# Loads and stores of a streaming kernel in one DMA queue instead of two

## The chip, the cores and the metric

The kernel runs on one core of one Trainium2 chip. The metric is device time in microseconds (us), the median of several runs. Before the change it is 168.21 us (three runs, 167.97 to 169.08). The change is judged by the same metric.

## The reference

A tensor `x` of 128 samples by 128 steps by 512 features (f32, 33.6 MB) is multiplied by a factor per sample and feature. The factor comes from a small network over the sample's condition vector (512 features):

```python
h = jax.nn.silu(cond @ W1.T + b1)
gate = jax.nn.sigmoid(h @ W2.T + b2)[:, None, :]
# a Haar transform of x over the steps, every coefficient times gate, the inverse transform: x * gate
x = x + (x + x * gate)          # = x * (2 + gate)
```

The transform is orthonormal and the gate does not depend on the step, so transform and inverse cancel, and what is left is `out = x * (2 + gate)`. `x` is read once and `out` written once.

## The kernel before, in words

`x` is cut into 16 chunks: two groups (`GROUPS`, 64 samples each) by eight (`SLOTS`) of 8 steps (`CHUNK_STEPS`). A sample's 128 steps are split over two partitions, so a chunk is 128 partitions by 8 steps by 512 features, 2,048 KB, with 16 KB in a row in each partition and in HBM. The tile `ring` has eight slots, one for each chunk of a group. A chunk is loaded into its slot, multiplied there in place, and stored from there. The second group uses the same eight slots again.

- SyncE (SP) issues the loads. First the weights and the condition rows (lines 100 to 102), then all eight loads of group 0 with no wait (line 104), then the eight loads of group 1 (line 109), the load of slot s after a wait for the store of slot s in group 0 (`chunk_stored[s]`).
- ScalarE (ACT) issues the two bias loads (lines 165 and 166), runs the sigmoids (lines 171 and 176), and then issues all sixteen stores (line 182), each after a wait for VectorE's count `chunk_scaled`. At its end it waits for the last stores (line 185).
- TensorE (PE) transposes the condition and the weights and makes the two matrix products (lines 126 to 160), and VectorE (DVE) copies between them and makes `factor` (line 211).
- VectorE then multiplies the sixteen chunks in order (line 218), each after its load has landed (`chunk_loaded[s]`), and counts up `chunk_scaled`.

Loads and stores so go into two DMA queues, one that SP fills (q1 in the profile) and one that ACT fills (q10). Within a queue the transfers are taken in the order of issue. Between the two nothing in the program orders them but the semaphores.

Of the kernel before, what the change touches and what calls it, by code (L numbers as in the profile page):

```python
# [1 line left out]

# [8 lines left out]
CHUNK_STEPS = 8  # L31
GROUPS = 2
SLOTS = 8
DMA_DONE = 16


def gated_residual_program(nc, x, cond, w1, b1, w2, b2, out):
    B, N, D = x.shape
    BLOCKS = D // P
    SAMPLES = B // GROUPS  # L40
    assert B == P and D == BLOCKS * P and N == GROUPS * SLOTS * CHUNK_STEPS and GROUPS >= 2

    x_parts = x.rearrange("(g q) (h n) d -> g (q h) n d", g=GROUPS, h=GROUPS)
    out_parts = out.rearrange("(g q) (h n) d -> g (q h) n d", g=GROUPS, h=GROUPS)

    with ExitStack() as ctx:
        def sbuf(name, shape):
            return ctx.enter_context(nc.sbuf_tensor(name, shape, F32))
# [4 lines left out]
        def sem(name):  # L53
            return ctx.enter_context(nc.semaphore(name))


        ring = sbuf("ring", [P, SLOTS, CHUNK_STEPS, D])

# [27 lines left out]
        gate_summed, gate_set, factor_set = sem("gate_summed"), sem("gate_set"), sem("factor_set")  # L86
        chunk_loaded = [sem(f"chunk_loaded{s}") for s in range(SLOTS)]
        chunk_scaled = sem("chunk_scaled")
        chunk_stored = [sem(f"chunk_stored{s}") for s in range(SLOTS)]

        block = ctx.enter_context(nc.Block())

        def chunk(parts, g, s):

            return parts[bass.ds(g, 1), :, s * CHUNK_STEPS:(s + 1) * CHUNK_STEPS, :].rearrange("g p n d -> (g p) n d")

        @block.sync
        def _(sp):

            sp.dma_start(w1_rows[:, :, :], w1.rearrange("(p t) k -> p t k", t=BLOCKS)).then_inc(w1_loaded, DMA_DONE)  # L100
            sp.dma_start(cond_rows[:, :], cond).then_inc(cond_loaded, DMA_DONE)
            sp.dma_start(w2_rows[:, :, :], w2.rearrange("(t p) k -> p t k", p=P)).then_inc(w2_loaded, DMA_DONE)
            for s in range(SLOTS):
                sp.dma_start(ring[:, s, :, :], chunk(x_parts, 0, s)).then_inc(chunk_loaded[s], DMA_DONE)
            with sp.Fori(1, GROUPS) as g:
                for s in range(SLOTS):

                    sp.wait_ge(chunk_stored[s], g * DMA_DONE)
                    sp.dma_start(ring[:, s, :, :], chunk(x_parts, g, s)).then_inc(chunk_loaded[s], DMA_DONE)

        @block.gpsimd
        def _(pool):
# [50 lines left out]
        @block.scalar  # L163
        def _(act):
            act.dma_start(b1_cols[:, :], b1.rearrange("(p t) -> p t", t=BLOCKS)).then_inc(b1_loaded, DMA_DONE)
            act.dma_start(b2_row[:, :], b2.rearrange("(a j) -> a j", a=1)).then_inc(b2_loaded, DMA_DONE)

            act.wait_ge(b1_loaded, DMA_DONE)
            act.wait_ge(hidden_summed, 1)
            for t in range(BLOCKS):  # L170
                act.activation(hidden_sigmoid[:, t, :], hidden_sum[:, t, :], ACT.Sigmoid,  # L171
                               bias=b1_cols[:, t:t + 1]).then_inc(sigmoid_set, 1)

            for g in range(GROUPS):
                act.wait_ge(gate_summed, g + 1)
                act.activation(gate[:, g, :], gate_sum[g][:, :], ACT.Sigmoid).then_inc(gate_set, 1)  # L176

            with act.Fori(0, GROUPS) as g:
                for s in range(SLOTS):

                    act.wait_ge(chunk_scaled, g * SLOTS + (s + 1))
                    act.dma_start(chunk(out_parts, g, s), ring[:, s, :, :]).then_inc(chunk_stored[s], DMA_DONE)

            for s in range(SLOTS):
                act.wait_ge(chunk_stored[s], GROUPS * DMA_DONE)

        @block.vector
        def _(dve):

# [51 lines left out]
```

## Time and profile before

| | us |
|---|---|
| median of the runs | 168.21 |
| runs, lowest to highest | 167.97 to 169.08 |
| span of the profiled execution | 166.7 |
| VectorE busy in it | 78.3 |
| TensorE busy in it | 23.7 |
| ScalarE busy in it | 3.6 |
| bytes moved by DMA | 69.47 MB, mean 417 GB/s |

The profiled execution is one run of the program, and its span goes from the first to the last instruction. The median of the runs is 1.5 us above it. Busy time of an engine is the time in which it executes, without waits and without the issuing of DMAs. The page divides the span into 40 slices, 4.17 us each, and gives for each slice the busy share of the 16 DMA engines and the GB/s that they moved. A chain of waits follows the work that ended last back from its end.

### The profile page before, as it was taken

What the parts mean: (1) busy time and instruction counts of PE and PEld (TensorE: products, weight loads), DVE (VectorE), ACT (ScalarE), POOL (GpSimd) and SP (SyncE); (2) the same over time, 40 slices, a digit from 0 to 9 for tenths busy, and PEclk for the clock granted to TensorE, in tenths of its full rate; (3) what the DMA queues carried; (4) which work ended last, traced back from release to release, by engine and by line L of the source; (5) the groups of instructions that cost most, each with busy time, mean ns of one, the idle gap of its engine ahead of it and who ended that gap; (6) DMA issues with size and microseconds to landing.
All of it is one profiled execution on the core that took longest, in us unless ns stands there. A gap on an engine that the chain in (4) does not pass through costs nothing.

```text
span 166.7 us, 361 instructions
## 1 busy us (share of the span) xinstructions
PE 23.7 (14%) x88; PEld 15.6 (9%) x88; DVE 78.3 (47%) x30; ACT 3.6 (2%) x7; POOL 0.8 (1%) x7
## 2 busy tenths in 40 slices
PE   0479619960000000000000000000000000000000
PEld 0479613320000000000000000000000000000000
DVE  0160180019999999997809154280915428000000
ACT  0000500110000000000000000000000000000000
POOL 2000000000000000000000000000000000000000
PEclk9999965997555555555555555555555555555555
DMA  5999999999999999999999999999999999999995
GB/s 167 313 457 440 421 421 429 433 437 433 413 437 429 429 437 440 425 425 429 437 429 437 433 425 433 429 433 433 437 433 425 433 429 429 437 433 433 429 429 236
DMA packets 5570, 69.47 MB, mean 417 GB/s; under 512 B 705, under 2 KB 705, under 8 KB 1346
## 3 DMA queue, kind: packets, MB, share of 16 engines
q1 hardware_dynamic: 3120, 35.91, 51.3%
q10 hardware_dynamic: 2450, 33.56, 47.1%
HBM read 35.92 MB, written 33.55 MB: 417 GB/s over the span
## 4 chain that ended last, share of the span: by engine, by line
DMA 41%; DVE 26%; PE 13%; ACT 2%; issue 2%; SPq 0%; DVEq 0%; ACTq 0%
DMA out<-ring 27%; DVE ring L218 22%; DMA ring<-in_x 11%; PE gate_sum L160 5%; PE hidden_sum L140 3%; DMA cond_rows<-in_cond 3%; PE turned L132 2%; PE gate_sum L157 2%; DVE w_t L208 1%; DVE hidden L201 1%; ACT L171 1%; ACT hidden_sigmoid L171 1%; PE turned_cond L126 1%; DVE factor L211 0%; DVE w_t L194 0%
## 5 line engine op out<-in xcount | busy, mean ns | idle before, releaser
L218 DVE TENSOR_TENSOR ring<-ring,factor 128x4096 f32<-128x4096 f32 x16 | 70.1, 4421 | 33.3 <-DMA ring<-in_x 33.0
L160 PE MATMUL gate_sum<-w_t,hidden 128*128 128x512 f32 x16 | 8.8, 702 | 0.0
L211 DVE TENSOR_SCALAR factor<-gate 128x1024 f32<-128x1024 f32 x1 | 0.7, 694 | 12.6 <-ACT gate L176 12.6
L140 PE MATMUL hidden_sum<-cond_t,w_t 128*128 128x128 f32 x32 | 5.5, 351 | 0.9 <-DVE w_t L194 0.9
L201 DVE SCALAR_TENSOR_TENSOR hidden<-hidden_sum,b_cols,hidden_sigmoid 128x256 f32<-128x256 f32 x4 | 1.7, 478 | 8.3 <-ACT hidden_sigmoid L171 8.3
L140 PEld LDWEIGHTS hidden_sum<-cond_t,w_t 128*128 128x128 f32 x32 | 5.3, 264 | 1.2 <-issue 1.2
L191 DVE COPY cond_t<-turned_cond 128x512 f32<-128x512 f32 x1 | 0.7, 692 | 7.8 <-PE turned_cond L126 7.8
L160 PEld LDWEIGHTS gate_sum<-w_t,hidden 128*128 128x128 f32 x16 | 3.5, 229 | 6.0 <-issue 6.0
L157 PE MATMUL gate_sum<-b_row,ones_row 1*128 1x512 f32 x4 | 3.2, 881 | 4.9 <-DVE w_t L208 4.9
L132 PE MATMUL turned<-identity,w_rows 128*128 128x128 f32 x16 | 3.6, 421 | 0.0
L132 PEld LDWEIGHTS turned<-identity,w_rows 128*128 128x128 f32 x16 | 3.4, 230 | 0.0
L194 DVE COPY w_t<-turned 128x512 f32<-128x512 f32 x4 | 2.8, 692 | 0.6 <-PE turned L132 0.6
L208 DVE COPY w_t<-turned 128x512 f32<-128x512 f32 x4 | 2.5, 681 | 0.0
L149 PE MATMUL turned<-identity,w_rows 128*128 128x128 f32 x16 | 2.1, 283 | 0.0
L126 PE MATMUL turned_cond<-identity,cond_rows 128*128 128x128 f32 x4 | 1.1, 428 | 6.6 <-DMA cond_rows<-in_cond 6.6
L149 PEld LDWEIGHTS turned<-identity,w_rows 128*128 128x128 f32 x16 | 2.0, 208 | 0.0
L171 ACT ACT_TABLE_LOAD x1 | 1.3, 1283 | 17.6 <-PE hidden_sum L140 17.6
L176 ACT ACTIVATE gate<-gate_sum 128x512 f32<-128x512 f32 x2 | 1.2, 597 | 15.5 <-PE gate_sum L160 15.5
L157 PEld LDWEIGHTS gate_sum<-b_row,ones_row 1*128 1x128 f32 x4 | 0.8, 244 | 5.8 <-issue 5.8
L126 PEld LDWEIGHTS turned_cond<-identity,cond_rows 128*128 128x128 f32 x4 | 0.7, 216 | 6.6 <-issue 6.6
L171 ACT ACTIVATE hidden_sigmoid<-hidden_sum,b_cols 128x128 f32<-128x128 f32 x4 | 1.1, 368 | 0.0
L117 POOL TENSOR_SCALAR_AFFINE_SELECT identity<-identity 128x128 f32<-128x128 f32 x1 | 0.3, 294 | 0.1
(6 smaller groups left out, 0.8 us busy)
## 6 DMA issues: line engine op xcount, KB each, us to landing
ring<-in_x SPq DMA_DIRECT2D x16, 2048.0 KB, 18.2
out<-ring ACTq DMA_DIRECT2D x16, 2048.0 KB, 34.8
w_rows<-in_L_cond_W SPq DMA_DIRECT2D x2, 1024.0 KB, 6.8
cond_rows<-in_cond SPq DMA_DIRECT2D x1, 256.0 KB, 5.3
b_cols<-in_L_cond_b ACTq DMA_DIRECT2D x1, 2.0 KB, 5.2
b_row<-in_L_cond_b ACTq DMA_DIRECT2D x1, 2.0 KB
```

Of the source, the lines that this page charges most:

```text
L126: last = pe.transpose(turned_cond[:, c * B:(c + 1) * B], cond_rows[:, c * P:(c + 1) * P], identity[:, :])
L132: last = pe.transpose(turned[c][:, t * P:(t + 1) * P], w1_rows[:, t, c * P:(c + 1) * P], identity[:, :])
L140: last = pe.matmul(hidden_sum[:, t, :], w1_t[:, c, t, :], cond_t[:, c, :], start=(c == 0), stop=(c == BLOCKS - 1))
L149: last = pe.transpose(turned[t][:, m * P:(m + 1) * P], w2_strided[:, m, t, :], identity[:, :])
L157: pe.matmul(gate_sum[g][:, :], ones_row[:, :], b2_row[:, :], start=True, stop=False)
L160: last = pe.matmul(gate_sum[g][:, :], samples, w2_t[:, t, :], start=False, stop=(t == BLOCKS - 1))
L171: act.activation(hidden_sigmoid[:, t, :], hidden_sum[:, t, :], ACT.Sigmoid, bias=b1_cols[:, t:t + 1]).then_inc(sigmoid_set, 1)
L176: act.activation(gate[:, g, :], gate_sum[g][:, :], ACT.Sigmoid).then_inc(gate_set, 1)
L194: dve.tensor_copy(w1_t[:, c, :, :].rearrange("k t p -> k (t p)"), turned[c][:, :]).then_inc(w1_t_set, 1)
L201: dve.scalar_tensor_tensor(out=hidden[:, t, :, :], in0=hidden_sum[:, t, :].unsqueeze(2).to_broadcast([P, B, GROUPS]), scalar=b1_cols[:, t: ...
L208: dve.tensor_copy(w2_t[:, t, :], turned[t][:, :]).then_inc(w2_t_set, 1)
L218: dve.tensor_tensor(ring[:, s, :, :], ring[:, s, :, :], factor_steps, ALU.mult).then_inc(chunk_scaled, 1)
```

## The change

All sixteen stores move from ACT's queue to SP's. SP issues them in a list written out in Python instead of a loop on the engine. For each chunk i it waits until chunk i is multiplied and issues its store. From the third store on, until all eight loads of group 1 are out, it then waits until store i - 2 has landed and issues the load that goes into that slot. The wait for the last stores moves from ACT to SP. ACT keeps the two bias loads and its activations. VectorE, TensorE and GpSimd are unchanged, and so are the sizes and number of the transfers.

```diff
+BEHIND = 2
@@ sync
             for s in range(SLOTS):
                 sp.dma_start(ring[:, s, :, :], chunk(x_parts, 0, s)).then_inc(chunk_loaded[s], DMA_DONE)
-            with sp.Fori(1, GROUPS) as g:
-                for s in range(SLOTS):
-
-                    sp.wait_ge(chunk_stored[s], g * DMA_DONE)
-                    sp.dma_start(ring[:, s, :, :], chunk(x_parts, g, s)).then_inc(chunk_loaded[s], DMA_DONE)
+            chunks = GROUPS * SLOTS
+            for i in range(chunks):
+                sp.wait_ge(chunk_scaled, i + 1)
+                sp.dma_start(chunk(out_parts, i // SLOTS, i % SLOTS),
+                             ring[:, i % SLOTS, :, :]).then_inc(chunk_stored[i % SLOTS], DMA_DONE)
+
+                j = i - BEHIND
+                if j >= 0 and j + SLOTS < chunks:
+                    sp.wait_ge(chunk_stored[j], DMA_DONE)
+                    sp.dma_start(ring[:, j, :, :],
+                                 chunk(x_parts, 1 + j // SLOTS, j % SLOTS)).then_inc(chunk_loaded[j], DMA_DONE)
+
+            for s in range(SLOTS):
+                sp.wait_ge(chunk_stored[s], GROUPS * DMA_DONE)
@@ scalar
-            with act.Fori(0, GROUPS) as g:
-                for s in range(SLOTS):
-
-                    act.wait_ge(chunk_scaled, g * SLOTS + (s + 1))
-                    act.dma_start(chunk(out_parts, g, s), ring[:, s, :, :]).then_inc(chunk_stored[s], DMA_DONE)
-
-            for s in range(SLOTS):
-                act.wait_ge(chunk_stored[s], GROUPS * DMA_DONE)
```

## Rows read from the trace of the kernel before

**Rows 1.** The page: span, busy time of the engines, DMA share and rate by slice.
```profile
span 166.7 us, 361 instructions
PE 23.7 (14%) x88; PEld 15.6 (9%) x88; DVE 78.3 (47%) x30; ACT 3.6 (2%) x7; POOL 0.8 (1%) x7
...
DMA  5999999999999999999999999999999999999995
GB/s 167 313 457 440 421 421 429 433 437 433 413 437 429 429 437 440 425 425 429 437 429 437 433 425 433 429 433 433 437 433 425 433 429 429 437 433 433 429 429 236
```

**Rows 2.** The page: DMA queues with packets, MB, share of the 16 engines.
```profile
q1 hardware_dynamic: 3120, 35.91, 51.3%
q10 hardware_dynamic: 2450, 33.56, 47.1%
```

**Rows 3.** The chain of waits, its last pieces: start us, length us, what.
```profile
72.72 45.41 DMA out<-ring
118.13 0.02 issue
118.15 18.24 DMA ring<-in_x
136.39 0.02 issue
136.41 4.42 DVE ring L218
```

**Rows 4.** Who waited for whom, VectorE and SP's queue: us in total, times, longest.
```profile
DVE ring L218 <- DMA ring<-in_x: 33.0, 7, 5.3
...
SPq L109 <- DMA out<-ring: 108.8, 8, 47.4
```

**Rows 5.** Three stretches: busy us by engine, TensorE clock, DMA share, GB/s.
```profile
16.00:42.00 26.00, 15.19 (x50) 7.47 (x48) 8.95 (x10) 3.62 (x7) 0.00 (x0) 0.82 1.00 427
62.00:134.00 72.00, 0.00 (x0) 0.00 (x0) 41.45 (x10) 0.00 (x0) 0.00 (x0) 0.50 1.01 431
144.00:162.00 18.00, 0.00 (x0) 0.00 (x0) 0.00 (x0) 0.00 (x0) 0.00 (x0) 0.50 1.01 432
```

**Rows 6.** The issues of line 104, and how long they took to land.
```profile
L104 SPq DMA_DIRECT2D ring<-in_x x8: 434/482/877, 2.1 to 6.3; - x8
...
DMA to landing us min/median/max: 13.1/28.1/46.9
```

**Rows 7.** The issues of line 109 and of line 182: duration ns, first and last start.
```profile
L109 SPq DMA_DIRECT2D ring<-in_x x8: 327/328/328, 54.3 to 118.2; - x8
...
L182 ACTq DMA_DIRECT2D out<-ring x16: 337/338/389, 42.4 to 141.0; - x16
```

**Rows 8.** VectorE in order of time, multiplies of line 218: start us, busy us.
```profile
37.79 39.11 DVE L218 TENSOR_TENSOR ring<-ring,factor 128x4096 f32<-128x4096 f32 x9 [0.33 <-DVE factor L211]
...
87.81 4.42 DVE L218 TENSOR_TENSOR ring<-ring,factor 128x4096 f32<-128x4096 f32 x1 [5.30 <-DMA ring<-in_x]
...
136.41 4.42 DVE L218 TENSOR_TENSOR ring<-ring,factor 128x4096 f32<-128x4096 f32 x1 [5.28 <-DMA ring<-in_x]
```

**Rows 9.** DMA in the last 3 us, in 40 slices of 0.075 us from 164.
```profile
GB/s 218 437 437 437 218 874 437 437 218 0 219 0 0 0 0 0 219 0 0 0 0 0 0 0 0 0 0 0 0 0 0 0 0 0 0 0 0 0 0 0
DMA packets 35, 0.31 MB, mean 104 GB/s; under 512 B 16, under 2 KB 16, under 8 KB 16
```

**Rows 10.** ACT's waits for the last stores, line 185: duration ns, first and last start.
```profile
L185 ACTq EVENT_SEMAPHORE  x4: 17/38/38, 151.6 to 166.2; - x4
```

## Prediction, made before the changed kernel was run

> **What bounds the kernel now.** I read the page first. VectorE is busy for 78.3 of 166.7 us and TensorE for 23.7, but the DMA share stands at 9 in every slice between the first and the last [rows 1]. So no compute engine sets the time. The 16 DMA engines do. Next come the queues: 35.91 MB in q1 and 33.56 MB in q10, together 98.4% of all the time that the 16 engines have in the span [rows 2]. The third view is the table of three stretches, chosen so that each shows one regime: loads alone in one queue (16 to 42 us), loads and stores side by side in two queues (62 to 134), stores alone in one queue (144 to 162). They moved 427, 431 and 432 GB/s at a DMA share of 1.00 to 1.01 [rows 5]. The reader should see that rate depends hardly at all on direction, or on whether one queue or two are served.
>
> The chain of waits confirms this in its own way. Its last long pieces are a store of 45.41 us, a load of 18.24 us and one multiply [rows 3]. A transfer of 2.097 MB takes 2.097 / 431 = 4.87 us when it has the engines to itself, so those pieces are mostly time spent standing in a queue. The waits say the same: VectorE waits 33.0 us for loads and SP waits 108.8 us for stores [rows 4], and neither wait leaves the DMA engines idle. They are consequences of the full DMA.
>
> **The fixed part.** The first slice moved at 167 GB/s, the second at 313, and the last at 236 [rows 1]. This start and end hold what the kernel loses against a steady rate. At the start stand the same loads of weights, biases and conditions in the same queues, and the change touches none of them. The last slice ends with the last store and its landing, which the change keeps too.
>
> **The change part by part.**
>
> *Who issues.* Sixteen issues of 0.34 us leave ACT and go to SP, where the same kind takes 0.33 us [rows 7]. SP then has 24 issues after the first eight loads, 24 x 0.33 = 8 us over more than 110 us. SP now waits 108.8 us [rows 4], and this is the cover. If it were gone the 8 us would still lie beside transfers of 4.87 us each. ACT has nothing left behind its gates, so no engine waits for it. I cost this at 0. The closing wait of line 185 moves from ACT to SP, with the same 0.04 us [rows 10]: 0.
>
> *The order of the transfers.* Call the group 0 loads L0 to L7, the stores S0 to S15, and the loads of group 1 N0 to N7. SP's queue becomes L0 to L7, S0, S1, S2, N0, S3, N1, S4, and so on to S9, N7, S10, then S11 to S15. I walk through it to find a place where the DMA engines could run dry. The first load lands at 2.1 + 13.1 = 15.2 us [rows 6], and the others follow at 2.097 / 427 = 4.91 us each, so L7 ends at 15.2 + 7 x 4.91 = 49.6. The first store is issued at 42.4 [rows 7], and VectorE delivers another every 39.11 / 9 = 4.35 us [rows 8], so S1 is issued at 46.7 and S2 at 51.1. S0 is in the queue 7 us before its turn. It runs from 49.6 to 54.4, S1 to 59.3, S2 to 64.1.
>
> *The new waits.* SP waits for S0 from about 51.4 to 54.4, and behind that wait stand N0 and S3. At that moment S1 and S2 are still in the queue, 9.7 us of work. SP issues N0 at 54.4 and S3 at 55.4, when chunk 3 is multiplied. In the same way N1 goes out at 59.3 with S2, N0 and S3 (14.6 us) before it, and from S2's landing at 64.1 on there are always four transfers, about 19.4 us, between the transfer that SP waits for and the load that it then issues. One wait only would have to be late by over 9.7 us, and the later ones by 14 to 19 us, before the engines had nothing. Loads of the second group: N0 ends at 64.1 + 4.9 = 69.0 and the next ones every 9.77 us, so N7 ends at 69.0 + 7 x 9.77 = 137.4. Now its multiply starts at 136.41 [rows 8]. Its product is ready at about 137.4 + 4.4 = 141.8 us, and S15's turn comes only after S10 to S14, at 137.4 + 5 x 4.86 = 161.7, so 20 us of cover remain. S10 itself needs chunk 10, which is multiplied before 95 us. No stall arises, and none disappears: the DMA engines were full before and are full after.
>
> *The rate.* What remains is whether the same bytes pass at the same rate. Now a pair of a load and a store takes (136.41 - 87.81) / 5 = 9.72 us [rows 8]. In the new order the two run one after the other, each at the rate of its own regime: 2.097 / 427 + 2.097 / 432 = 4.91 + 4.85 = 9.76 us [rows 5], 0.04 us more. Over the eight pairs that is 0.3 us. If the group 1 loads run at the mixed rate instead, it is 0.
>
> *The turns.* The trace of before shows no change from stores to loads inside one queue, and the new order has 17: one at L7 to S0, and two for each of N0 to N7. The nearest row below is the mixed stretch, in which load and store packets of two queues share each DMA engine at a DMA share of 1.01 and 431 GB/s [rows 5], so those turns cost nothing there. It could not be much less than nothing, since a share of 1.01 leaves no gap that could be closed, and the best regime is 432. The far end is an engine that lets the writes of one kind be confirmed before it goes on with the other: the last packet starts in the slice at 164 + 16 x 0.075 = 165.2 us [rows 9], though packets of the bulk stop near 164.7, and the wait for the last store starts at 166.2 [rows 10], which leaves at most 1.0 us for the rest of a packet and the confirmation. Of that 1.0 us about 0.6 is the packet (16 KB on one engine, 16,384 B / (431 / 16 GB/s) = 0.61 us), so 0.4 us is a turn's dearest price: 17 x 0.4 = 6.8 us. I take 0, since the mixed stretch is the same engines doing the same kinds of packets in turn, and only the queue that they come from differs.
>
> The Trainium skill speaks against it at this point. Its page "DMA: Bandwidth & Descriptors", section "Anatomy of one DMA", puts a fixed cost of about 2 us on a DMA, most of it the receipt of the write by the target memory. If each turn exposed that, the kernel would take 17 x 2 = 34 us more, some 202 us by an estimate from that page. The stretches with one queue show transfers back to back at 427 and 432 GB/s, so between transfers of one direction this case's trace does not show that cost. Between directions no row shows it either way.
>
> **The sum.** 166.7 + 0 (issue) + 0 (waits) + 0.3 (rate) + 0 (turns) = 167.0 us in the profiled execution. The median of the runs stands 1.5 us above the span now, so 168.5 us.
>
> **The rivals.**
>
> *A: turns in one queue cost time (slower).* Place: the 17 boundaries between loads and stores. For it speaks that no row shows such a boundary. Against it stands the mixed stretch. At the dearest price the time is 168.5 + 6.8 = 175.3 us, at a quarter of that, 0.1 us a turn, 170.2. It decides (over 1%) from about 0.08 us a turn on. The likelier part is the cheap end.
>
> *B: SP's waits in one list starve the queue (slower).* A late store would hold back N and S together, which two queues do not do. It needs a landing later than 9.7 us at the first wait. Before, N0 was issued at 54.3 [rows 7], so S0 landed 12 us after its issue even beside the loads. If the queue did run dry once for 3 us, the time would be 171.5. Nothing in the profile points to it.
>
> *C: one queue is served faster (faster).* The first ten slices (41.7 us) moved 395 GB/s in the mean, 16.5 MB [rows 1], so 53.0 MB are left. At the 432 of the stores' stretch instead of 431 they would take 53.0 / 432 = 122.7 us against 123.0, 0.3 us less: 167.9 us. To be faster by over 1% (1.7 us) they would need 53.0 / 121.3 = 437 GB/s, which no stretch of [rows 5] shows.
>
> *D: the change does nothing to the order.* If loads and stores of one queue still overlapped freely, the pair would stay at 9.72 us and the time at 168.2. This falls within the forecast.
>
> **How the numbers follow.** Forecast (with D, and the small gain of C): 0.85. A: 0.08. B: 0.03. C by over 1%: 0.03, and 0.01 for something else on the slower side. About 1% is what a measurement of this kernel can tell from no change. The forecast's part lies within 1%, and so does 0.01 of A, its prices under 0.08 us a turn. So faster 0.03, same 0.86, and slower 0.07 + 0.03 + 0.01 = 0.11. The range starts at 167.4, below C's 167.9 by half a microsecond for the spread of the runs, and reaches to 170.2, A at 0.1 us a turn. What is left out is mostly A and B above it. I predict 168.5 us.
>
> **What would show it.** Right: all bulk packets in q1 and the DMA share at 9 in all slices but the first and last; about 431 GB/s between 62 and 134 us; the multiplies of group 1 starting 9.7 to 9.8 us apart, the last near 137.5; SP's issues of group 1 loads from 54.4 to about 113 (118.2 now); the end at 167. A shows as a lower rate in the stretch of alternating transfers, with pairs longer than 9.8 us, while loads alone and stores alone keep theirs. B shows as single slices below 9 near 55 to 65 us. The prediction is wrong if the pair's time moves by more than 0.1 us, or if a gap opens in the DMA.

## The result: slower by 1.3%

| | before | changed |
|---|---|---|
| median, us | 168.65 (4 runs) | 170.93 (4 runs) |
| lowest to highest, us | 167.97 to 169.85 | 170.57 to 171.52 |
| span of the profiled execution, us | 166.7 | 168.8 |

The changed kernel takes 1.0132 times the time of the kernel before, 95% interval 1.0094 to 1.017. I had forecast no change at 168.5 us and put 170.2 at the end of the range. The spans show nearly the same step as the medians: 168.8 - 166.7 = 2.1 us. Against the forecast span of 167.0 us the profiled execution is 1.8 us late. The other 0.6 us of the 2.4 us between forecast and median come from the distance between span and median, which I had taken as 1.5 us and which is 2.1 us here, because the profiled execution was the fastest of the four.

The page of the changed kernel, with DMA share and rate in 40 slices of 4.22 us, and then the two queues, answers to [rows 1, 2]:

```profile
span 168.8 us, 303 instructions
...
DMA  4899999999999999999999999999999999999992
GB/s 169 293 444 435 427 427 431 431 431 435 431 431 431 431 419 431 419 435 423 435 423 431 419 423 431 423 431 423 435 431 427 431 435 431 423 435 435 435 431 101
...
q1 hardware_dynamic: 5424, 69.47, 97.3%
q10 hardware_dynamic: 146, 0.00, 0.1%
```

All chunks pass through q1 now. The share still reads 9 from the third slice to the 39th, and no slice shows a hole. Two places differ from before: nine slices from the 15th to the 35th drop to 419 or 423, and the last slice moved at 101 GB/s, where it was 236 [rows 1]. The same three stretches as in [rows 5], with busy us by engine, clock, DMA share and GB/s:

```profile
16.00:42.00 26.00, 14.77 (x32) 5.92 (x30) 9.37 (x11) 3.15 (x7) 0.00 (x0) 0.78 1.01 430
62.00:134.00 72.00, 0.00 (x0) 0.00 (x0) 41.02 (x10) 0.00 (x0) 0.00 (x0) 0.50 1.01 428
144.00:162.00 18.00, 0.00 (x0) 0.00 (x0) 0.00 (x0) 0.00 (x0) 0.00 (x0) 0.50 1.01 433
```

The stretch in which loads and stores alternate lost 3 GB/s against [rows 5], 0.7% of 72 us or 0.5 us. The other stretches lost nothing. The rest shows only at the very end. The DMA view of the last microseconds, 165 to 169 in 40 slices of 0.1 us, changed kernel:

```profile
DMA  0033070003070003070003070000000000000000
GB/s 0 0 164 164 0 328 0 0 0 164 0 328 0 0 0 164 0 328 0 0 0 164 0 328 0 0 0 0 0 0 0 0 0 0 0 0 0 0 0 0
DMA packets 29, 0.21 MB, mean 53 GB/s; under 512 B 16, under 2 KB 16, under 8 KB 16
```

and the same window of the kernel before:

```profile
DMA  0030000000000000000000000000000000000000
GB/s 0 0 164 0 0 0 0 0 0 0 0 0 0 0 0 0 0 0 0 0 0 0 0 0 0 0 0 0 0 0 0 0 0 0 0 0 0 0 0 0
DMA packets 9, 0.02 MB, mean 4 GB/s; under 512 B 8, under 2 KB 8, under 8 KB 8
```

Here is the thing to read. A slice of 0.1 us with 164 GB/s is one 16 KB packet that starts in it, and 328 is two. Before, one packet starts after 165 us. In the changed kernel a pattern of three packets repeats every 0.6 us up to 167.4. So three of the 16 DMA engines still work through their part of the last store while thirteen are done. A share averaged over 16 engines hides three late ones until the end, when nobody covers for them.

The trace also holds the moment at which each of the 16 engines reports its part of a transfer. From these moments come the tables below. The last store, S15, in us:

```
before    first 165.03, 13th 165.56,                    last 166.17
changed   first 165.41, 13th 166.22, 14th 168.10, 15th 168.29, 16th 168.30
```

The first of the engines is 0.4 us later than before, the last 2.1 us. VectorE shows the lateness where it arises. Multiplies of group 1 in order of time, changed kernel (start us, busy us, idle before and releaser):

```profile
79.36 4.42 DVE L199 TENSOR_TENSOR ring<-ring,factor 128x4096 f32<-128x4096 f32 x1 [2.88 <-DMA ring<-in_x]
89.11 4.42 DVE L199 TENSOR_TENSOR ring<-ring,factor 128x4096 f32<-128x4096 f32 x1 [5.33 <-DMA ring<-in_x]
99.63 4.43 DVE L199 TENSOR_TENSOR ring<-ring,factor 128x4096 f32<-128x4096 f32 x1 [6.10 <-DMA ring<-in_x]
...
139.16 4.42 DVE L199 TENSOR_TENSOR ring<-ring,factor 128x4096 f32<-128x4096 f32 x1 [5.32 <-DMA ring<-in_x]
```

Each multiply waits for the last of the 16 engines. The last one starts at 139.16 us, where I had forecast 137.5. From 89.11 to 139.16 the mean interval is 10.01 us, against 9.72 before [rows 8], and one interval (89.11 to 99.63) is 10.52.

### The profile page after: what moved, and what is told of

It reads as the page before. It is cut to its first block, busy times and chain, and to the rows that moved or that the text cites. A ratio compares the mean times of both kernels' runs of the same rounds, so it can differ in the third digit from the quotient of the medians.

```text
span 168.8 us, 303 instructions
## 1 busy us (share of the span) xinstructions
PE 23.1 (14%) x88; PEld 14.1 (8%) x88; DVE 78.2 (46%) x30; ACT 3.6 (2%) x7; POOL 0.8 (0%) x7
## 4 chain that ended last, share of the span: by engine, by line
DMA 58%; PE 12%; DVE 11%; ACT 2%; issue 1%; SPq 1%; DVEq 0%; ACTq 0%
DMA out<-ring 40%; DMA ring<-in_x 15%; DVE ring L199 8%; PE gate_sum L150 6%; DMA cond_rows<-in_cond 3%; PE hidden_sum L130 2%; PE gate_sum L147 2%; PE turned L122 1%; DVE w_t L189 1%; DVE hidden L182 1%; DVE w_t L175 1%; ACT L161 1%; ACT hidden_sigmoid L161 1%; PE turned_cond L116 1%; DVE factor L192 0%
## 5 line engine op out<-in xcount | busy, mean ns | idle before, releaser
L150 PE MATMUL gate_sum<-w_t,hidden 128*128 128x512 f32 x16 | 10.5, 815 | 0.0
L150 PEld LDWEIGHTS gate_sum<-w_t,hidden 128*128 128x128 f32 x16 | 4.0, 260 | 6.8 <-issue 6.8
L130 PE MATMUL hidden_sum<-cond_t,w_t 128*128 128x128 f32 x32 | 3.8, 277 | 1.0 <-DVE w_t L175 1.0
L130 PEld LDWEIGHTS hidden_sum<-cond_t,w_t 128*128 128x128 f32 x32 | 3.6, 192 | 1.2 <-issue 1.2
L122 PE MATMUL turned<-identity,w_rows 128*128 128x128 f32 x16 | 3.1, 379 | 0.0
L139 PE MATMUL turned<-identity,w_rows 128*128 128x128 f32 x16 | 2.1, 283 | 0.0
```

The costliest lines, as they stand in the source:

```text
L122: last = pe.transpose(turned[c][:, t * P:(t + 1) * P], w1_rows[:, t, c * P:(c + 1) * P], identity[:, :])
L130: last = pe.matmul(hidden_sum[:, t, :], w1_t[:, c, t, :], cond_t[:, c, :], start=(c == 0), stop=(c == BLOCKS - 1))
L139: last = pe.transpose(turned[t][:, m * P:(m + 1) * P], w2_strided[:, m, t, :], identity[:, :])
L150: last = pe.matmul(gate_sum[g][:, :], samples, w2_t[:, t, :], start=False, stop=(t == BLOCKS - 1))
```

## The experiments

All times are ratios to the kernel before on the same chip, with 95% intervals. S, L and N name stores, group 0 loads and group 1 loads as in the prediction. The spread of a transfer is the time from the first to the last of the 16 engines reporting it, each read from one profiled execution. The edits are shown against the changed kernel and shortened: `store(i)` is the wait for chunk i and the issue of its store, `load(j)` the wait for store j and the issue of the load into its slot.

### Is it the queue or the moment of the issues?

```diff
 # SP: the stores only. ACT, after its gates:
+            for j in range(SLOTS):
+                act.wait_ge(chunk_scaled, j + BEHIND + 1)
+                act.wait_ge(chunk_stored[j], DMA_DONE)
+                act.dma_start(ring[:, j, :, :], chunk(x_parts, 1, j)).then_inc(chunk_loaded[j], DMA_DONE)
```

> SP issues the stores, ACT issues the group 1 loads, with the same waits and so at the same moments as in the changed kernel, but in a queue of their own. Theory one (the single queue costs the time): as before the change, ratio 1.000, span 166.7, and the 16 engines finish the last store within 1.2 us of each other. Theory two (the moment at which the loads are issued, or the wait for the store two back, costs it): ratio 1.013, span 168.8, as in the changed kernel, last landing spread over 2.9 us.

Measured: 0.9955 (0.9902 to 1.0008), span 166.2, spread of the last store 0.8 us. The lost time is back. The conditions for each issue are those of the changed kernel, but the moments came out otherwise, because the stores land later beside loads: the group 1 loads were issued from 54.2 to 118.5 us, nearly as before the change, instead of 54.6 to 114.4. So this run alone does not part the queue from the moment of the issues. Two later kernels do, which put an SBUF tile on one side: with one queue and loads issued from 53.8 to 112.5 us and from 55.1 to 113.7 us, they lost nothing either ("Which side of memory does it take?").

### Fewer turns in the one queue

Three kernels keep the one queue on SP and group the transfers otherwise. The first:

```diff
+            for i in range(SLOTS): store(i)
+            for j in range(SLOTS): load(j)      # waits for chunk_stored[j]
+            for i in range(SLOTS, 2 * SLOTS): store(i)
```

> One queue on SP, but all eight stores of group 0 first, then all eight loads of group 1, then the stores of group 1: 3 turns between loads and stores instead of 17. If each turn, or each load that lies between stores, costs time: ratio at most 1.003, last landing spread about 1.3 to 1.7 us. If one queue costs it without regard to the turns (issuer, ring): ratio 1.013 as in the changed kernel.

Measured: 0.998 (0.9925 to 1.0035), span 166.7. The spread is 1.4 us at L7, 1.3 at N7 and 1.4 at the last store. One queue as such costs nothing. What costs is the alternation in it. The second kernel takes the loads in pairs:

```diff
-                j = i - BEHIND
-                if j >= 0 and j + SLOTS < chunks: load(j)
+                j = i - BEHIND - 1
+                if j >= 0 and j % 2 == 0 and j < SLOTS:
+                    load(j)
+                    load(j + 1)
```

> One queue on SP, the group 1 loads in pairs between pairs of stores: 9 turns instead of 17. A cost for each turn: (9 / 17) of the 2.1 us lost, ratio about 1.007. A loss that late engines suffer through the whole time in which loads lie between stores, whatever the number of turns: ratio 1.013.

Measured: 1.0074 (1.0011 to 1.0138), span 168.0. The spread grows from 1.3 us (N0) to 1.6 (N1), 2.3 (N3), 2.7 (N5), and stays there. By the median this fits a price per turn, though the interval also reaches the 1.013 of the changed kernel. The spread says where the time goes: it grows by 0.3 to 0.6 us at N1, N3 and N5, and by 0.1 us or less at N2, N4, N6 and N7. Where it grows, the load is the second of its pair, the one with a store right behind it. The third, run later, uses blocks of four:

```diff
+            for half in range(2):
+                for i in range(4): store(4 * half + i)
+                for i in range(4): load(4 * half + i)
```

> One queue, stores and group 1 loads in blocks of four: 5 turns, two of them from group 1 loads to stores (the changed kernel has eight such turns and 17 in all). If the late engines lose 0.1 to 0.6 us at each turn from loads back to stores: landing spread 1.3 growing to 1.5 to 2.3, ratio 1.000 to 1.006. If the skew grows with the time from the first group 1 load on: 2.9 us and 1.013.

Measured: 0.9995 (0.9968 to 1.0023), span 166.9, the spread 1.1 us at L7, 1.2 at N3, 1.4 at N7, 1.5 at S15. The time from the first group 1 load on is not what makes the spread grow. A price per turn is not refuted by it, since blocks of four have only two group 1 loads with a store right behind them, N3 and N7, where the changed kernel has eight.

### Another issuer

```diff
 # the changed kernel's list word for word, sp. replaced by act., the group 0 loads too;
 # the weight loads stay on SP
```

> The list of the changed kernel word for word, but issued by ACT into ACT's queue, the loads of group 0 too. One queue with alternating transfers costs the time: ratio 1.013, spread of the last landing about 2.9 us. SP or its queue costs it: ratio 1.000 to 1.003. The start may move by some tenths of a us, because weights and chunks are then in two queues.

Measured: 1.0357 (1.0271 to 1.0443), span 173.3. The time of this run says little about the queue, for a reason that I had put at some tenths of a microsecond. Who waited for whom in it:

```profile
PEld turned L123 <- DMA w_rows<-in_L_cond_W: 11.9, 1, 11.9
```

The weights in SP's queue now share the DMA engines with the chunks in ACT's. TensorE waits 11.9 us for them, the gate is late, and so is the first store. The DMA view from 40 to 60 us has a hole of about 3 us where the loads are through and no store is there yet:

```profile
DMA  9998999998999986100000939999399995799993
```

The hole is not all of it, since between 62 and 74 us the kernel moved only 355 GB/s, which I did not take apart. But its spreads are of use. Behind the hole the 16 engines start nearly level, with a spread of 0.2 us at S0, and in the alternation it still grows, to 0.7 us at N0, 1.3 at N4 and 2.3 at the last store. The engines need not be out of step at the start for it.

The next kernel has the weights first in ACT's queue as well, and the two bias loads on SP:

```diff
-            sp.dma_start(w1_rows ...); sp.dma_start(cond_rows ...); sp.dma_start(w2_rows ...)
+            act.dma_start(w1_rows ...); act.dma_start(cond_rows ...); act.dma_start(w2_rows ...)
-            act.dma_start(b1_cols ...); act.dma_start(b2_row ...)
+            sp.dma_start(b1_cols ...); sp.dma_start(b2_row ...)
```

> Everything that SP issues in the changed kernel (weights, chunks, stores, waits) is issued by ACT in the same order, and the two bias loads by SP, so the weights come first in the same queue again. If the ring with alternating transfers costs the time, whoever fills it: 1.013 plus what the late gate costs (ACT also runs the sigmoids, and its issues come before them). If ACT's queue itself is dearer, as the 1.036 of the earlier run may mean: above 1.025 with the first store landing before 55 us.

Measured: 1.0108 (1.0057 to 1.016), span 169.0. S0 begins to land at 53.1 us, and the spread grows from 1.2 us at L7 to 1.6 (N0), 2.7 (N2) and 3.4 (N4), and stays at 3.1 to 3.4. Whoever fills the queue, it is the same loss.

### More turns, and other neighbours

First the control: each chunk goes in two transfers of four steps, one behind the other.

```diff
+            HALF = CHUNK_STEPS // 2          # 8 KB rows, 1,024 KB a transfer
+            # S_i half 0, S_i half 1, wait for S_(i-2), N_(i-2) half 0, N_(i-2) half 1
```

> The changed kernel with each chunk moved by two transfers of 1,024 KB, one behind the other, so the number of turns between loads and stores stays 17. It is the control for the next run. If only the turns cost: ratio 1.013 and a last landing spread near 2.9 us, plus what 8 KB packets cost by themselves, up to 0.5%.

Measured: 1.0171 (1.011 to 1.0231), span 170.4, the spread of a half 1.0 us at N0, 2.8 at N3, 3.2 at the end. Again it grows at the half that has a store right behind it: 1.0 us at the first half of N1 and 1.5 at the second, 1.5 and 2.2 in N2, 2.2 and 2.8 in N3. Then the same pieces in turn:

```diff
+            # S_i half 0, wait for S_(i-2), N_(i-2) half 0, S_i half 1, N_(i-2) half 1
```

> The same 1,024 KB transfers, but half a store, half a load, half a store, half a load: 33 turns instead of 17. If the cost goes with the number of turns, as 3, 9 and 17 turns gave 0.998, 1.007 and 1.013: about 1.026 to 1.030. If it goes with the time in which loads lie between stores: as the control, within 0.3%.

Measured: 1.0092 (1.0066 to 1.0118), span 168.0. This overturned a price per turn. With 33 turns instead of 17 the spread is 1.0 us at L7 and never above 1.1 from there to the last store, so no engine falls behind. What is left of the loss fits the price of 8 KB rows, though no kernel with two queues and 8 KB rows was run. The stretch 16 to 42 us, which has only group 0 loads, shows it in both kernels, here this one:

```profile
16.00:42.00 26.00, 14.42 (x30) 5.72 (x29) 9.72 (x11) 2.95 (x7) 0.00 (x0) 0.77 1.01 422
```

422 GB/s against 427 to 430 with 16 KB rows is 1.2 to 1.9% of the rate. In the other two stretches this kernel moved 427 and 428 GB/s, where the kernel before had 431 and 432, and the whole kernel lost 0.9%.

The next run keeps 17 turns and changes which store stands beside which load, and doubles the queue ahead of each:

```diff
-BEHIND = 2
+BEHIND = 4
```

> BEHIND 4 instead of 2: 17 turns again, but each load stands beside another store (chunk 4 + k and 5 + k of the output instead of 2 + k and 3 + k) and has twice the queue ahead of it. Turns as such: ratio 1.013. If the queue ran short at a wait, or if the addresses of neighbouring loads and stores met in memory: another ratio, 1.000 for the first of these.

Measured: 1.0126 (1.0095 to 1.0157), span 168.9. The spread grows from 0.9 us at N0 to 1.4 (N1), 1.7 (N2), 2.5 (N3), 2.9 (N4) and 3.2 (N7). Neither a short queue at the waits nor this one pairing of addresses is the cause.

The changed kernel itself was run again beside later ones.

> The changed kernel as it is, once more, beside the next three on one chip. Ratio 1.010 to 1.016. Last store: most engines finish within 1 us, two or three of the 16 engines 2 to 3 us after them, if the late engines are the cause and not an accident of one execution.

Measured: 1.0077 (1.0033 to 1.0121), span 169.4. The spread goes from 1.0 us at L7 to 1.3 (N0), 2.2 (N2), 3.2 (N3), 3.7 at the end. This time one engine is 3.7 us after the first and four are 1.3 to 1.8 us after it. The interval overlaps that of the first measurement, and the ratio is lower than I had expected.

A way to have short runs and 16 KB rows at once would be halves by partitions:

```diff
+            HALF = P // 2
+            sp.dma_start(ring[h * HALF:(h + 1) * HALF, s, :, :], chunk(x_parts, g, s)[h * HALF:(h + 1) * HALF])
```

> Every chunk moved as two transfers of 64 partitions, stores and loads alternating by halves (33 turns). Rows stay 16 KB, unlike the step halves. If short runs in one direction keep the engines together (step halves at 33 turns: spread stayed 1.1 us) and their 0.9% came from the 8 KB rows: ratio 0.997 to 1.003, spread 1.1 to 1.3. If transfers of 64 partitions reach fewer engines or ports at once, it is slower by far more than 1%, in all stretches alike.

Measured: 1.2779 (1.2739 to 1.282), span 215.0. The stretch 16 to 42 us, loads alone:

```profile
16.00:42.00 26.00, 16.67 (x48) 7.80 (x47) 7.47 (x10) 3.62 (x7) 0.00 (x0) 0.80 1.01 214
```

The 16 engines read busy at a share of 1.01 and move half the bytes. But that holds for the first part of the kernel only. Later stretches of the same execution, loads and stores in turn and then stores alone:

```profile
140.00:160.00 20.00, 0.00 (x0) 0.00 (x0) 9.41 (x3) 0.00 (x0) 0.00 (x0) 0.50 1.01 430
192.00:202.00 10.00, 0.00 (x0) 0.00 (x0) 0.00 (x0) 0.00 (x0) 0.00 (x0) 0.50 1.01 433
```

From about 120 us on, the same transfers of 64 partitions moved at the full rate. So half the rate belongs to the group 0 loads, one half behind the other, and not to every transfer of 64 partitions. What changes in between was not taken apart, and the kernel as a whole is out. It also shows that transfers of 1,024 KB with 16 KB rows can run at full rate, which leaves the 8 KB rows for the loss of the step halves.

### Which side of memory does it take?

In the next kernel the eight group 1 loads read another SBUF tile instead of HBM.

```diff
-                    sp.dma_start(ring[:, j, :, :], chunk(x_parts, 1 + j // SLOTS, j % SLOTS))
+                    sp.wait_ge(w1_loaded, DMA_DONE)
+                    sp.dma_start(ring[:, j, :, :].rearrange("p (r t) k -> p r (t k)", r=2),
+                                 w1_rows[:, :, :].rearrange("p t k -> p (t k)").unsqueeze(1)
+                                 .to_broadcast([P, 2, BLOCKS * D]))
```

> The eight group 1 loads copy w1_rows (8 KB a partition, twice) from SBUF into the slot instead of reading x from HBM, so the second half of the output is other data; order, waits, size and number of transfers are those of the changed kernel, with 8 KB rows in these eight. If the late engines lose their time in reads from HBM while the others already write to HBM: spread stays at about 1.3 us from the first to the last store. If any turn inside one queue does it, whatever is read: it grows to about 2.9 us. The rate may differ for its own reasons, so the spread of the landings decides, not the ratio.

Measured: 0.9994 (0.9971 to 1.0017), span 166.5. The spread is 0.7 us at L7, at every group 1 load and at the last store. Reads from HBM are needed for the loss. These eight loads have 8 KB rows, but those alone do not keep the engines together: the step halves at 17 turns had them too, and their spread grew to 3.2 us. Then the other side, stores S2 to S9 into SBUF, and its control:

```diff
+            def to(i):                                   # the control: always the output in HBM
+                if not 2 <= i < 2 + SLOTS: return chunk(out_parts, i // SLOTS, i % SLOTS)
+                return spare[:, :, :] if i % 2 else w_rows ...   # w1_rows and w2_rows, one tile
+                # wait for chunk_stored[i - 2], then S_i into to(i), then N_(i-2)
```

> The eight stores that lie between the group 1 loads (S2 to S9) copy their chunk into other SBUF tiles instead of HBM, so those chunks are missing in the output. SP waits for the store two back before it issues the next store, not after (else the changed kernel's order of transfers, 17 turns, same sizes, 16 KB rows). The group 1 loads read x from HBM. If it takes both sides of HBM, reads of late engines against writes of early ones: the landing spread stays at its first value, 0.7 to 1.4 us, to the last store. If a load from HBM behind any other transfer in the queue is enough: it grows to 2.5 to 3.7 us as in the changed kernel.

Measured: 1.0 (0.9982 to 1.0018), span 167.1.

> The same program as the one before it, its waits too, but with all stores to HBM, so it computes the reference. It should behave as the changed kernel: spread growing to 2.5 to 3.7 us, ratio 1.007 to 1.016. If the moved wait itself changes something, its spread or ratio will say so, and the run before has to be read against it.

Measured: 1.0132 (1.0097 to 1.0168), span 169.7. The spreads of both, beside those of the changed kernel, of the run before them and of the two-queue form, in us:

```
                                       L7   N0   N1   N3   N5   N7   S15
changed kernel                        1.3  1.5  1.7  2.3  2.6  2.9  2.9
loads from HBM, stores to HBM (ctrl.) 1.0  1.4  2.0  3.1  3.8  3.9  3.9
loads from HBM, S2-S9 into SBUF       1.0  1.1  1.1  1.1  1.1  1.1  1.0
group 1 loads from SBUF, stores HBM   0.7  0.7  0.7  0.7  0.7  0.7  0.7
two queues, HBM both ways             0.9  0.7  0.7  0.8  0.8  0.8  0.8
```

With the same order, turns and waits, the end looks like this in the control and then in the kernel with the stores into SBUF (165 to 169 us, 40 slices):

```profile
DMA  3033070030370030370030003030003030000000
...
DMA packets 34, 0.29 MB, mean 74 GB/s; under 512 B 16, under 2 KB 16, under 8 KB 16
```

```profile
DMA  7370033000000000000000000000000000000000
...
DMA packets 23, 0.11 MB, mean 29 GB/s; under 512 B 16, under 2 KB 16, under 8 KB 16
```

The loss takes both, loads that read HBM and stores that write HBM, taken in turn from one queue. With either one replaced by an SBUF tile, nobody falls behind. The traffic with HBM alone does not explain it, since the two-queue form has all of it and keeps its engines together.

### Does the two-queue form beat both kernels?

The kernel of the first experiment again, in five rounds.

> Stores in SP's queue, group 1 loads in ACT's, timed in five rounds against the kernel before: is it faster than both kernels? Its first timing gave 0.9955 with an interval over 1. If it is only the kernel before with the queues exchanged: 0.998 to 1.002. If its closer landings (0.8 us against 1.1) are worth something: 0.995 to 0.998.

Measured: 0.9969 (0.9951 to 0.9987), span 166.2. Stores in SP's queue and group 1 loads in ACT's has the lowest ratio of all forms that compute the reference, 0.3% under the kernel before. Against the block of eight (0.998) the intervals overlap. Its last report comes at 165.8 us, 0.4 us earlier than before. It begins to report its last store at 165.0 us like the kernel before, with a spread of 0.8 us where that one had 1.1. This is a small gain whose mechanism I did not take apart.

## Why the prediction was wrong, point by point

**What bounds the kernel: right, but read too coarsely.** The DMA engines set the time before and after. I read a mean over 16 engines as if it were each of them. A transfer is done when its last engine is done, and the end of the kernel likewise.

**Issues: right.** SP's 24 issues have grown longer, up to 0.91 us where four come close together, 10.1 us in all instead of the 8 that I had forecast, and are hidden as forecast. Issues of the stores in the changed kernel (duration ns, first and last start):

```profile
L89 SPq DMA_DIRECT2D out<-ring x16: 332/450/914, 41.8 to 143.6; - x16
```

**Waits: right.** Forecast for the group 1 loads were issues from 54.4 to about 113, measured were 54.6 to 114.4, and the queue never ran dry (rival B did not happen). With BEHIND 4 the queue ahead is twice as long and the time the same.

```profile
L95 SPq DMA_DIRECT2D ring<-in_x x8: 339/340/340, 54.6 to 114.4; - x8
```

**Rate: right for most of the engines.** I had put 0.3 us on the alternation of the two regimes. The first engine reports the last store at 165.41 instead of 165.03, 0.4 us later, and the thirteenth 0.7 us later. By the first engine's reports of N0 and N7 (67.82 and 136.22 us) a pair takes 9.77 us, as forecast.

**Turns: the step that failed.** I priced the 17 turns at 0, because in the stretch with two queues the engines take load and store packets by turns at a share of 1.01. That row does not bear on the case. With two queues, loads and stores are mixed in every microsecond: in each piece of 1.2 us between 72 and 112 us, 25 to 72% of the large packets that start are q1's. In one queue an engine reads 128 KB (2,048 KB / 16) and then writes 128 KB, and the 16 engines do so a little out of step. The measured price is 1.8 us, the 168.8 us of the span less the 167.0 that I had forecast for it with 0.3 us for the rate. The signs that I had named for rival A came true: the alternating stretch fell from 431 to 428 GB/s, the pairs grew from 9.72 to 10.01 us, and loads alone and stores alone kept their rates. Rival A had the right place, sign and size, 1.8 / 17 = 0.11 us a turn, and I gave it 0.08. But its mechanism, a pause of every engine at every turn, is refuted as well: thirteen engines lose 0.4 to 0.7 us in all, and 33 shorter turns build up no lag. So it is luck that the measured 0.11 us lies so near the 0.1 us at which I had priced A. The loss falls on two to five of the 16, which drop back unevenly at the group 1 loads, the last of them by up to 1.0 us at a load, until it is 2.3 to 3.9 us behind the first. The dearest price, 6.8 us, was built on the confirmation of the last write, a thing that no run singled out. I should have seen that a regime without any row of its own deserves more than 8 parts in 100, and that the kernel has 17 turns over which a small price adds up.

**The rule of the Trainium skill** that I weighed, the fixed cost of some 2 us of the page "DMA: Bandwidth & Descriptors", section "Anatomy of one DMA", is not paid at the turns: 202 us by it, 170.9 measured. That section gives the cost for transfers issued by GpSimd, which I had left out, and the queues here are filled by SyncE and ScalarE. The Trainium skill's advice in the section "Rules for kernel authors" of the same page, that spreading DMAs over issuing engines does not help bandwidth, does not hold to the last percent where loads and stores alternate: with the same transfers, the changed kernel took 1.0132 times the time of two queues. With blocks of four or eight in one queue this case agrees with it within the noise (0.9995 and 0.998).

**What stays open.** Shown is that it takes alternation in one queue, reads from HBM and writes to HBM in it, and runs of about 2,048 to 4,096 KB; halves in turn, runs of 1,024 KB, cost nothing of this kind. Argued only is how: late engines that still read HBM while the others already write are slowed by those writes, and so get later. Packets of 16 KB that took over 640 ns instead of 611 speak for it. The changed kernel has 48 of them, all near the end of a group 1 load (they start at most 2.5 us before the first engine reports it and before the last one does), and the kernel before has 3. The count follows the loss through the other kernels with 16 KB rows (the first of the two on ACT and the partition halves apart, which have other losses): 59 in the control with stores to HBM, 40 with four behind, none in the block of eight, in both runs of the two-queue form and in the kernels that use an SBUF tile, and 3 in blocks of four. With pairs there are 29, of them 17 at N3, 10 at N5 and one each at N1 and N7, which are the loads with a store right behind them. That the slow packets are what the spread is made of remains argued. Against it, as far as it goes, stands that the turn from L7 to S0, with the same spread, never made the spread grow, nor did halves of 1,024 KB taken in turn. Why short runs are harmless, and which engines are the late ones, was not found. Long runs may be harmless only because they have few turns: one group 1 load with a store right behind it in the block of eight, two in the blocks of four, where the spread did grow by 0.2 us at N7.

## What to carry to other kernels

Where loads from HBM and stores to HBM overlap at full DMA rate, give each direction its own queue. If they must share one, put them in long blocks (four or eight transfers of 2,048 KB cost nothing that could be measured here). Where the DMA share reads full, look at the last microseconds in fine slices and at what the slowest engine does before you call two orders of the same bytes equal. A regime that the trace doesn't show deserves a real chance in the forecast, however near its nearest row looks.

## What the runs showed of the hardware

- One DMA queue that alternates transfers of 2,048 KB from HBM and to HBM lets two to five of 16 DMA engines fall behind, the last of them 2.3 to 3.9 us behind the first. Two queues with the same transfers keep them within 0.6 to 2.2 us, within 0.8 to 1.1 at the end.
- Group 0 loads in two transfers of 64 partitions, one behind the other, ran at 214 GB/s, those over 128 partitions at 430, both with all engines reading as busy. Later in the same kernel such transfers ran at 430 to 433 GB/s.
- Rows of 8 KB instead of 16 KB cost 1.2 to 1.9% of the rate in loads alone, 422 against 427 to 430 GB/s.
- Weights in a queue beside the chunks instead of ahead of them kept TensorE waiting 11.9 us and held back the first store.
